# Four groups of edges share each run of eight records, kept in four areas that are added when read back: 814 tiles in place of 842

## What is computed

```python
xn = layernorm(x)
agg = segment_sum(edge_weight[:, None] * xn[dst], src, 6250)      # 100,000 edges
x = x + (agg @ gnn_W.T + gnn_b) + linear_attention(xn)            # Wq, Wkv, Wproj
h = layernorm(x)
combine = top2_softmax(h @ Wg.T + bg)                             # 8 experts
x = x + sum_e combine[e] * (relu(h @ W1[e].T + b1[e]) @ W2[e].T + b2[e])
```

## Time and profile before

| | us |
|---|---|
| median of 3 runs | 2117.31 |
| lowest, highest | 2112.32, 2119.97 |
| the profiled execution, whole | 2114.13 |
| its span in the profile | 2112.1 |

### The profile page before, as it was taken

The page is one execution under the profiler, slowest core; times in us unless marked ns, Lnnn a source line. Parts: engine busy times, 40 slices in busy tenths (PEclk is TensorE's granted clock), DMA queues, the critical chain, the costliest instruction groups (busy, mean ns, idle before and its releaser), DMA issues. The chain is left out here.

```text
span 2112.1 us, 51620 instructions
## 1 busy us (share of the span) xinstructions
PE 1706.0 (81%) x15598; PEld 1323.3 (63%) x15598; DVE 1599.7 (76%) x3345; ACT 1454.9 (69%) x4121; POOL 1319.7 (62%) x1257
## 2 busy tenths in 40 slices
PE   6677638888888789888976666662799999999998
PEld 3456526666666577777754344441677777777776
DVE  8899729888888899998888888897355555555554
ACT  6565438888788788888788888774556566566554
POOL 4488857777777777777777777760244444444443
PEclk8899859999999999999999999955799999999999
DMA  5022235555555544444433355452122222332231
GB/s 166 32 78 83 70 110 158 156 158 156 159 157 153 158 138 123 124 125 124 116 106 102 101 151 167 137 178 76 48 48 49 49 47 46 50 50 46 48 48 30
DMA packets 136768, 217.67 MB, mean 103 GB/s; under 512 B 32502, under 2 KB 93024, under 8 KB 136386
## 3 DMA queue, kind: packets, MB, share of 16 engines
q0 software_dynamic: 64160, 138.35, 26.0%
q1 hardware_dynamic: 65990, 69.65, 10.8%
q10 hardware_dynamic: 6364, 6.40, 0.9%
HBM read 173.49 MB, written 41.77 MB: 102 GB/s over the span
## 5 line engine op out<-in xcount | busy, mean ns | idle before, releaser
L978 POOL DMA_INDIRECT misc<-z_d,consts x842 | 810.0, 962 | 273.3 <-issue 166.1
L1214 DVE SCALAR_TENSOR_TENSOR acc<-ps,consts,acc 128x512 f32 x842 | 629.8, 748 | 87.4 <-PE ps L1301 68.6
L1001 ACT ACTIVATE misc<-misc 128x256 f16<-128x256 f16 x900 | 404.4, 498 | 83.9 <-DVE misc L1081 76.6
L1299 PE MATMUL ps<-misc 128*128 128x256 f16 x1124 | 308.5, 274 | 125.4 <-ACT rec L1001 42.5
L1808 ACT ACTIVATE misc<-ps,misc 128x128 f32<-128x128 f32 x840 | 239.5, 368 | 239.7 <-PE ps L1773 163.9
L1849 POOL DMA_INDIRECT out<-misc,pos x105 | 166.3, 1584 | 288.9 <-ACT misc L1873 253.0
L1773 PE MATMUL ps<-misc,big 128*128 128x128 f16 x1680 | 327.4, 220 | 0.0
L1771 PE MATMUL ps<-misc,big 128*128 128x128 f16 x1680 | 327.0, 220 | 0.1
L1772 PE MATMUL ps<-misc,big 128*128 128x128 f16 x1680 | 326.7, 219 | 0.0
L1788 PE MATMUL ps<-big,rec 128*128 x840 | 319.7, 381 | 0.1
L1301 PE MATMUL ps<-misc 128*128 128x256 f16 x1124 | 309.3, 275 | 0.0
(11 more groups left out here) (339 smaller groups left out, 3808.2 us busy)
## 6 DMA issues: line engine op xcount, KB each, us to landing
big<-in_w2T SPq DMA_DIRECT2D x60, 256.0 KB, 2.9
misc<-z_d,consts POOLq DMA_INDIRECT x842
big<-xT_d SPq DMA_DIRECT2D x98, 128.0 KB
big<-in_w1T SPq DMA_DIRECT2D x32, 256.0 KB, 2.9
tok_d<-misc SPq DMA_DIRECT2D x50, 132.0 KB, 1.9
xT_d<-misc SPq DMA_DIRECT2D x49, 128.0 KB, 1.8
z_d<-misc SPq DMA_DIRECT2D x49, 128.0 KB, 1.7
acc<-in_x SPq DMA_DIRECT2D x6, 896.0 KB
```

The lines of the kernel that those rows point to most:

```text
L978: e.indirect_dma_start(out=rows[n % RB], out_offset=None, in_=c.z_d, in_offset=bass.IndirectOffsetOnAxis(ap=idx[u][:, k:k + 1], axis=0)).t ...
L1001: e.activation(hot[n % HG][:, half, :], same[n % OG], ACT.Copy, scale=near[n // UG % 3][:, t % UG, 1 + half:2 + half]).then_inc(s_hot, 1)
L1214: e.scalar_tensor_tensor(out=rows_of, in0=out_ps[tile % BG], scalar=c.gain, in1=rows_of, op0=ALU.mult, op1=ALU.add).then_inc(s_add, 1)
L1299: e.matmul(o, w[:, 0, at], z[:, 0:D], start=True, stop=False)
```

## The change

Groups are joined by fours (`AR` = 4). Group i writes its records to area i % 4 of `rec_d`, and the four groups of a join share runs: the second group begins in the run in which the first one stopped, at the next free slot. In each area the other groups' slots of a shared run hold zeros, so the four areas can be added to get the records. Partial runs are now lost once per join and block, 7 x 25 times, not 28 x 25 times: 12,653 runs, `ETM` = 814 tiles, `ET` = 816 (34 turns of 24 tiles, before 36).

- Blanks are zeros. The DMAs that write them are seven as before but each writes all four areas, four times the bytes, and one more writes 128 zero rows at the head of `z_d`. All rows of `z_d` move by 128, and the index field (times four, plus 128) is written complete in `rank`. POOL's L304 goes. On read-back a maximum with the partition's number gives a blank its row, one of the 128 zero rows.
- DVE's chain that finds the runs is longer: nine instructions on 28 to 84 columns in place of four, one more after it (`offset`), and one more ahead of `base` (`first_at`).
- SP reads the areas back inside `rank`, two DMAs for each, when the last scatter of that area has landed. POOL's scatters and everything else in the sorting loop keep their number and order.
- In `collect` PE adds the four areas in PSUM: 112 matmuls against the identity in place of 28 transposes, into fp32 banks.
- In `graph` the weight chunks come two in every five tiles, not one in every three: tiles 642 to 721 and 728 to 807.

```diff
 KG, RPT = SC // RUN, P // RUN
-RUNS = (E + NG * NB * (RUN - 1)) // RUN
+AR = 4
+RUNS = (E + NG // AR * NB * (RUN - 1)) // RUN
...
-            e.wait_ge(s_spread, 1)
+            e.wait_ge(s_zero, 1)
             blank = zeros.bitcast(F16)
             for t in range(0, ET, P):
                 k = min(P, ET - t)
-                e.dma_start(c.rec_d[t * RPT:(t + k) * RPT, :].rearrange("(t s) w -> t (s w)", s=RPT),
-                            blank[0:k, :]).then_inc(s_blank, 16)
+                e.dma_start(areas[t:t + k], blank[0:k, :].rearrange("p (a w) -> p a w", a=1).to_broadcast(
+                    [k, AR, P * PC])).then_inc(s_blank, 16)
+            e.dma_start(c.z_d[0:P, :], blank).then_inc(s_blank, 16)
...
+            whole_tiles = ET // P
+            for m in range(AR):
+                e.wait_ge(s_sc[m], 16 * KG * (NG // AR))
+                e.dma_start(c.loaded[m][:, 0:whole_tiles, :], areas[0:whole_tiles * P, m, :].rearrange(
+                    "(r t) w -> t r w", t=P)).then_inc(s_areas, 16)
+                e.dma_start(c.loaded[m][0:ET - whole_tiles * P, whole_tiles, :],
+                            areas[whole_tiles * P:ET, m, :]).then_inc(s_areas, 16)
+            e.wait_ge(s_areas, 32 * AR)
...
-            v.link(e.tensor_scalar(runs_i[:, 0:NG], grouped(upto)[:, :, GT - 1], RUN - 1.0, None, ALU.add))
-            v.link(e.tensor_scalar(runs_i[:, NG:2 * NG], runs_i[:, 0:NG], 3, None, ALU.logical_shift_right))
-            v.link(e.tensor_copy(fresh_runs, runs_i[:, NG:2 * NG]))
-            v.link(e.tensor_tensor_scan(runs_before, ones, fresh_runs, 0.0, ALU.mult, ALU.add))
+            v.link(e.tensor_tensor_scan(within, joined, grouped(upto)[:, :, GT - 1], 0.0, ALU.mult, ALU.add))
+            v.add(e.tensor_scalar(runs_i[:, 2 * NG:3 * NG], within, RUN - 1.0, None, ALU.add))
+            v.link(e.tensor_tensor(ahead, within, grouped(upto)[:, :, GT - 1], ALU.subtract))
+            v.add(e.tensor_scalar(runs_i[:, 0:NG], ahead, 0.0, None, ALU.add))
+            v.link(e.tensor_scalar(runs_i[:, NG:2 * NG], ahead, RUN - 1.0, None, ALU.add))
...
+            v.add(e.tensor_tensor(fresh_runs, runs_q[:, 2 * NG:3 * NG], runs_q[:, 0:NG], ALU.subtract))
+            v.link(e.tensor_tensor(opened, runs_q[:, 2 * NG:3 * NG], runs_q[:, NG:2 * NG], ALU.subtract))
+            v.link(e.tensor_tensor_scan(runs_before, ones, opened, 0.0, ALU.mult, ALU.add))
...
-                e.dma_start(loaded[r][0:k, :], c.rec_d[r * P * RPT:(r * P + k) * RPT, :].rearrange(
-                    "(t s) w -> t (s w)", s=RPT)).then_inc(s_load, 16)
...
-            e.wait_ge(s_load, 16 * TR)
             for k in (1, 0, 2, 3):
                 for r in range(TR):
                     n = min(P, ET - r * P)
-                    l = e.transpose(parts[k][:, r * P:r * P + n], matrix(loaded[r], P, PC)[0:n, :, k], c.ident16[0:n, 0:n])
+                    for m in range(AR):
+                        l = e.matmul(parts[k][:, r * P:r * P + n], matrix(c.loaded[m][0:n, r, :], P, PC)[:, :, k],
+                                     c.ident16[0:n, 0:n], start=m == 0, stop=m == AR - 1)
...
-    turns, LOOPS, B0, PACE, EVERY = -(-ETM // UG), ET // (2 * UG), 13, 6, 3
+    turns, LOOPS, B0, PACE, SPLIT = -(-ETM // UG), ET // (2 * UG), 13, 6, 5 * CN // 2
...
-            if 0 <= n - split_at[layer] < EVERY * CN:
-                return layer, (n - split_at[layer]) // EVERY, (n - split_at[layer]) % EVERY
+            d = n - split_at[layer]
+            if 0 <= d < SPLIT:
+                m = (2 * d + 1) // 5
+                return layer, m, d - 5 * m // 2
```

More of the change, by code:

```diff
@@ L168, in rank @@
     dummies, first_run, fresh_runs, runs_before, delta, ones = (big.take(NG) for _ in range(6))
-    runs_i = big.take(2 * NG, I32)
+    within, ahead, opened, offset, first_at, joined = (big.take(NG) for _ in range(6))
+    runs_i, runs_q = (big.take(3 * NG, I32) for _ in range(2))
     inreal, tiles_f, end = (big.take(2) for _ in range(3))
@@ L178, in rank @@
     eps = big.take(2)
+    lift = big.take(1)
+    src_at = big.at
     src, dst, wgt = (big.take(EC, I32) for _ in range(3))
@@ L191, in rank @@
     assert ring.at <= NB * EC // 2
+    TR = -(-ET // P)
+    late = Arena(c.big, 32768)
+    late.at = ring.at
+    assert ring.at + TR * P * 2 <= NB * EC // 2 + NB * P // 2 and TR * P * 2 <= 3 * EC
+    c.loaded = [matrix(at(0, TR * P * 2).bitcast(F16), TR, P * PC) for at in (
+        lambda a, n: c.big[:, mask_at:mask_at + n], lambda a, n: c.big[:, blk_at:blk_at + n],
+        lambda a, n: c.big[:, src_at:src_at + n], lambda a, n: late.take(n))]
     prod32 = [p.bitcast(I32) for p in prod]
@@ L231, in rank @@
     S = lambda name: c.sem("rank_" + name)
-    s_src, s_load, s_wz, s_blank, s_out, s_spread = map(S, ("src", "load", "wz", "blank", "out", "spread"))
+    s_src, s_load, s_wz, s_blank, s_out, s_areas = map(S, ("src", "load", "wz", "blank", "out", "areas"))
     s_x = [S(f"x{k}") for k in range(XC)]
@@ L392, in _ @@
             v.add(e.tensor_tensor(base, upto, counts[:, 0:EC], ALU.subtract))
+            v.add(e.scalar_tensor_tensor(out=offset, in0=runs_q[:, 0:NG], scalar=-float(RUN), in1=ahead, op0=ALU.mult, op1=ALU.add))
             e.wait_ge(s_runs, 1)
@@ L760, in collect @@
     misc = Arena(c.big, 32768)
+    misc.at = 24576
     TR = -(-ET // P)
-    loaded = [misc.take(P * PC, F16) for _ in range(TR)]
     q_i, dst_i = (misc.take(ET, I32) for _ in range(2))
-    parts = [c.bank[k][:, :].bitcast(F16)[:, 0:ET] for k in range(PC)]
+    parts = [c.wide[k][:, 0:ET] for k in range(PC)]
     S = lambda name: c.sem("collect_" + name)
-    s_load, s_blk, s_tr, s_v, s_q, s_w = map(S, ("load", "blk", "tr", "vector", "q", "w"))
+    s_blk, s_tr, s_v, s_q, s_w = map(S, ("blk", "tr", "vector", "q", "w"))
     marks = edges(c)
```

49 lines of the change are left out of this document (27 added, 22 removed).

## The result

| | before | after |
|---|---|---|
| median, us | 2116.34 (4 runs) | 2086.79 (4 runs) |
| lowest, highest | 2112.32, 2119.97 | 2084.09, 2088.98 |
| the profiled execution, whole | 2114.13 | 2084.09 |
| its span in the profile | 2112.1 | 2082.3 |

The changed kernel takes 0.9859 of the time of the one before, with a 95% interval of 0.9842 to 0.9875: 29.6 us less. The forecast was 2088 us. The span (first to last instruction of the profiled execution) is 29.8 us shorter, and the sum of the prediction was -29.8.

A forecast was written before the change was run, and what follows sets the result against it. POOL's own gather pace, 1.253 us a tile, was taken as the bound. -35.1 + 0 + 1.1 - 0.75 + 5.0 = -29.8 us took the profiled 2114.1 to 2084.4 us, median 2087.6, forecast 2088 us, range 2082 to 2096.

The forecast's parts named there:

- if the first gather starts after 309 us: Start of the graph stage: a sign that the prediction is wrong; the first gather was expected at 304.5 us.
- What bounds the kernel: Graph stage: POOL's own gather pace, 1.253 us a tile, is the bound; no wait for PE exceeds 0.3 us.
- Gathers: Graph stage: 28 fewer gathers at 1.253 us each, -35.1 us.
- Weight chunks: Graph stage, chunks two in five tiles: POOL stays last and covers the denser work, 0 us (-1.6 to +3).
- if they come with each chunk: Weight stretches: the 9.8 us of longer gathers stay, since there are 64 chunks as before; the branch taken, 0.
- with each tile: Weight stretches: if longer gathers come by the tile, 32 tiles fewer would save 1.6 us; the branch not taken.
- Reload and blanks: ACT's wait for the last chunk's load, up to 3.1 us, and the zero-writing DMAs, 21.6 us: both covered, 0.
- DVE's chain: In `rank`: nine instructions replace four and two more follow, delaying the whole sorting loop, +1.1 us (0.8 to 1.8).
- Reading back: End of `rank`: areas 0 to 2 read under scatters, area 3 after the last; -0.75 us (-1.5 to +3).
- lands at 281.20 + 2.4: End of the sorting loop: the last scatter lands 2.4 us after its start, at 283.6.
- at most the 4.4 us that 1024 KB took: Read-back of an area: reading 816 KB takes at most 4.4 us, so each is done before the next begins.
- Turning: In `collect`: 112 matmuls take 9.2 us, PE starting at half clock and then speeding up; +5.0 us (+4 to +7.1).

The follow-up runs named there:

- the kernel of 814 tiles without areas: Kernel before with two weight chunks in five tiles and the tile count set to 814: 2074.46 us, ratio 0.9813; on a slower chip 2291.55 us, 0.9818.
- first profile: Profile of the unedited changed kernel from the recorded pair, beside the kernel before; the profiled execution took 2084.09 us.
- second: Profile of the changed kernel run again unedited, on another chip beside the kernel before: 2084.76 us, ratio 0.9855.
- third: Profile of the changed kernel run unedited once more, on a further chip, from its slowest run (2089.6 us); median 2083.92 us, ratio 0.9852.
- The two kernels that hold reads back: Changed kernel with all areas read after the last scatter landed: 2304.57 us, ratio 0.9875; with only area 2's read held until then: 2083.4 us, 0.9853.
- one area alone: Changed kernel with 28 turning matmuls of one area for 112, the other three areas' records left out: 2295.38 us, ratio 0.9846.
- The early turning: Changed kernel with PE adding areas 0 to 2 inside `rank`, leaving 28 matmuls to `collect`: 2078.04 us, ratio 0.9829; run again on another chip 2085.28 us, 0.9862.
- the denser chunks: Kernel before with weight chunks two in five tiles, 842 tiles and no areas: 2334.77 us, ratio 0.9999.

## Why the prediction was right, and where its parts were not

The forecast, 2088 us, was 1.2 us from the measured median. The profiles of the changed kernel split its difference to the one profile of before into these parts. The last column is the kernel of 814 tiles without areas. (Each part is rounded by itself.)

| part, us | forecast | first profile | second | third | no areas |
|---|---|---|---|---|---|
| start of the last scatter | +1.1 | -1.2 | +3.5 | +6.8 | -2.4 |
| from there to PE's start | -0.75 | +2.2 | +2.1 | +2.1 | -0.1 |
| from there to the first gather | +5.0 | +4.8 | +4.6 | +5.5 | +0.3 |
| first gather to last | -35.1 | -34.6 | -37.1 | -38.1 | -37.4 |
| last gather to the end | 0 | -1.1 | -2.2 | -0.6 | -1.2 |
| span | -29.8 | -29.8 | -29.0 | -24.3 | -40.8 |

One sign of being wrong that the prediction named did come: "if the first gather starts after 309 us". It starts at 305.0, 309.4 and 313.5 us. The first row of the table is why. The end of the sorting loop moves by 8 us with the same program, so that sign did not test the theory. The distance behind the last scatter does, 24.6 to 25.5 us, where the forecast's parts give 22.2.

**What bounds the kernel: right.** POOL's gathers are the pace before and after. No wait is longer than the gap, and a tile is worth a step of POOL. The kernel with 814 tiles and dense chunks shows it on the third chip. On the first chip, where POOL waits up to 2.0 us, it shows only that a tile is worth the distance between two gathers.

**Gathers: right in kind, 1.6 us too small.** 35.1 us was the plain tiles' pace. Nine profiles with 814 tiles, on chips where steps are 1.27 us, show the stage 34.6 to 38.8 us shorter, 36.7 in the mean. Part of it is the next term, and under 1 us is the median gather, 946 ns in most of them and 947 before. In the first profile it was 949 ns, and over 814 gathers the 2 ns took back nearly 2 us. Gathers run a little over the plain pace in the first 350 tiles too: summed one by one it is 2.7 us before and 2.7 to 5.2 us in the nine. I had not looked there, and what makes them longer no run shows.

**Weight chunks: 0 forecast, a gain measured.** Before, gathers were over their median by 58 ns for 96 tiles and 46 ns for 96, 10.0 us. After, it is 45 ns and 27 ns for 80 each, 5.8 us, and 5.1 to 7.7 us in the eight profiles with two chunks in five tiles. My step "if they come with each chunk" chose the wrong branch, and "with each tile" was right; its -1.6 us was even too small, as far as one profile of before can tell. The Trainium skill, GPSIMD Engine Reference, section 8 Key points, was what I leaned on for the wrong branch. It says that GpSimd contends with DVE instructions that read two SBUF operands. The rows don't refute that, but they don't show a price by the chunk either: with a chunk in half of the tiles a gather is no longer than in two fifths (994 and 972 ns against 994 and 976). No run here took L1180 away by itself, so what lengthens the gathers is open.

**Reload and blanks: right at 0.** ACT waited 2.1 us for the last chunk's load, where it had been 0.63 ("up to 3.1" in the forecast), and it was covered: POOL's longest wait for PE stayed 0.3 us to the last tile. The zeros took SP 12.7 us, not the 21.6 us of "four times that" and one more, all of it under cover.

**DVE's chain: +1.1 forecast, +1.8 measured**, at the upper bound. In the other two profiles of the changed kernel the chain takes 9.9 and 10.3 us, and in the three others without areas 8.4 to 8.6. From scan to L421, with nine steps for four, it is 3.95 us, where it was 3.17. The two further steps (`offset` and `first_at`) add 0.7 us, 0.27 of it idle. These are 1.5 us where I had 1.1. The last 0.3 us was in no term: two large operations took 1.35 and 1.26 us that took 0.97 and 0.98 before, beside one that took 0.61 and not 0.94. Whether it gets through to the scatters can't be read from one pair: the first scatter starts at 92.1, 92.4 and 94.6 in the three profiles, at 92.8 in the one of before with its fallen clock, and at 90.5 in the third chip's kernel without areas. Over all profiles the last scatter starts 2.6 us later with areas (283.7 against 281.1 in the mean), but the spread is too wide for ten against four to price it.

**Reading back: -0.75 forecast, +2.1 to +2.2 measured. This is the step that failed.** The forecast that a scatter "lands at 281.20 + 2.4" took the median landing of a scatter in quiet. Area 2's read, issued up to 1.4 us ahead of the last scatter, makes that landing 4.1 to 4.9 us. The two kernels that hold reads back have 2.2 us. In the first profile (4.4 against 2.4) that is 2.0 us. The other 1 us is the read: "at most the 4.4 us that 1024 KB took" was no bound, since 816 KB took 5.1 us, and the way from there to PE's start 1.4 us and not 1.1. The kernel before had the better row for it: there 5.17 us pass from the issue of the first read of 864 KB to PE's start (289.85 - 284.68), with the records in one piece. So the areas' layout in DRAM, pieces of 1 KB with the other areas' between them, need not be what made the read long; no run tested it by itself. By these rows nearly all of the +2.2 us against the kernel before is the late landing. The value lies within the bounds that I kept (-1.5 to +3), and the reason for the upper one was named there. I took the wrong end.

**Turning: right.** 112 matmuls took 8.73 us (9.2 forecast). The windows of PE in the kernel after show the clock at its lower level for the first 4 us and then rising:

```profile
293.00:295.00 2.00, 2.00 (x22) 1.74 (x20) 0.50 0.00 0
295.00:297.00 2.00, 2.00 (x35) 1.88 (x33) 0.97 0.00 0
```

22 stand in 2 us at 0.50 and 35 in 2 us at 0.97, which is 91 and 57 ns each. Some two or three reach over an edge and stand in two windows, so I estimate 100 and 63 ns. The part measured +4.8 us against my +5.0, and one area alone gives 4.3 of it. The Trainium skill's 55.6 ns for a warm matmul of 128 columns (TensorE: Matmul & The Clock Gate, Part 1) is below what this window shows, and the 71 ns that I took is above it, by about as much.

**The whole.** The areas cost 9.5 us by the medians of the third chip and I had 5.35, and 28 tiles with dense chunks bring 39.9 us (36.6 to 42.7 by the interval) and I had 35.1. By these medians two errors of 4 to 5 us cancel. But both differences hold the same median of 2074.46 us, so a kernel without areas that was quick by chance makes both too large at once, and its last scatter did start 2.4 us early. The distances within the traces are off by less: from the last scatter to the first gather the changed kernel takes 6.7 to 7.6 us more, not 4.25, and the stage is 36.7 us shorter in the mean, not 35.1. The total came out in all three sessions (-29.6, -29.6, -30.5 us by the medians); only the third has the two sides apart. The first profile hid both, as its gathers were slow by 2 ns and its sorting loop ended early.

**A version that beats both.** The kernel of 814 tiles without areas does, but only for inputs whose records fit, so it is a measure and no replacement. The early turning was at 0.9829 once and at 0.9862 once, the changed kernel at 0.9855 and 0.9852 beside it. It takes 4 us off the path in every trace. Whether its median is lower stays open.

## What to carry to other kernels

Split a sum at two or three marks that every trace has (here the last scatter, the first and the last gather) and check each piece: a total that fits can hide two misses of several us. Before you price a wait for a landing at its median, look for what else moves on the DMA engines at that moment: here a read issued up to 1.4 us earlier nearly doubled it. And where a stretch ahead of the mark ends anywhere within 8 us from run to run, one profile of each kernel cannot price a microsecond behind it; keep to distances between marks that follow each other closely.

## What the hardware showed that I had not expected

- Beside the read of 816 KB a scatter of 128 runs of 64 bytes landed after 4.1 to 4.9 us (eight profiles), and with no read beside it after 2.2 (two profiles).
- In two of fourteen profiles two scatters each took POOL 4.1 to 5.1 us, and in the other twelve none took over 2.83 us. Those two are the ones in which the sorting loop ends at 288 us.
- 816 KB read in two halves from two queues took 5.0 us, and from one queue 5.1.
- The same kernel took 2114 us on two chips of the experiments and 2335 us on the other, with gathers 1.52 us apart and not 1.27. There POOL waits for PE 219 times, up to 2.0 us, while its own gathers take the same 949 ns in the median.
- TensorE's clock was at its lower level from 44 to 48 us in the profile of before and at its upper one in that of after, and in that of the denser chunks, whose `rank` is the code of before. In the 4 us ahead PE had been busy for 2.5, 3.2 and 2.7 us.
- Gathers beside the weight chunks got no longer when the chunks were packed closer: 1005, 994 and 994 ns in the first layer, 993, 976 and 972 in the second.
